# New hand-written instruction orders for a four-stage block on one core, with Pool masking three tiles and stores on two queues

## The reference, cut to what matters

```python
x = x + _L0_attn_a_ref(_layernorm(x), w1, w2, b2, sparse_mask)
x = x + _L0_ffn_ref(_layernorm(x), weight, bias, centroids, assignments)
x = x + _L0_attn_b_ref(_layernorm(x), Wqkv, bqkv, Wo, bo)
x = x + _L0_ffn_ref(_layernorm(x), weight, bias, centroids, assignments)

# stage 1
attn = jnp.einsum('ds,td->st', w1, w2) * sparse_mask
y = jnp.einsum('bds,st->bdt', x, attn) + b2;  return gelu(y)
# stages 2 and 4
dots = softmax(x @ centroids.T / 0.1)
hits = dots > 0.01
query_sel = jnp.any(hits, axis=1)      # per token
cluster_sel = jnp.any(hits, axis=0)    # over ALL tokens of all batches
row_sel = cluster_sel[assignments]     # per output feature
out = jnp.where(query_sel[:, None] & row_sel[None, :], x @ weight.T + bias, 0)
# stage 3: single-head attention with D = 128, then Wo and bo
```

## Time and profile before

| | us |
|---|---|
| median of 3 executions | 277.5 |
| lowest, highest | 277.13, 278.13 |
| profiled execution, its own time | 277.1 |
| its span in the profile | 275.3 |
| PE busy | 268.8 |
| DVE, ACT, Pool busy | 195.7, 176.6, 158.9 |
| granted TensorE clock, mean | 0.999 of full |

### The profile page before, as it was taken

The page is one execution under the profiler, slowest core; times in us unless marked ns, Lnnn a source line. Parts: engine busy times, 40 slices in busy tenths (PEclk is TensorE's granted clock), DMA queues, the critical chain, the costliest instruction groups (busy, mean ns, idle before and its releaser), DMA issues.

```text
span 275.3 us, 4427 instructions
## 1 busy us (share of the span) xinstructions
PE 268.8 (98%) x1396; PEld 224.5 (82%) x1396; DVE 195.7 (71%) x410; ACT 176.6 (64%) x358; POOL 158.9 (58%) x192
## 2 busy tenths in 40 slices
PE   8899999999999999999999999999999999999994
PEld 7787888888888888789988888888888888887673
DVE  3989988505926867775399796788349475967996
ACT  3855886455476785449899888778555567575400
POOL 4892988265495481289896993970730438113730
PEclk9999999999999999999999999999999999999999
DMA  7999064800000000000000000000000000000087
GB/s 248 368 374 317 11 228 158 304 0 0 2 0 0 2 0 2 2 0 0 2 0 0 4 1 0 0 2 0 2 2 0 0 2 0 1 2 0 19 305 287
DMA packets 10247, 18.23 MB, mean 66 GB/s; under 512 B 1201, under 2 KB 1969, under 8 KB 10225
## 3 DMA queue, kind: packets, MB, share of 16 engines
q1 hardware_dynamic: 10080, 17.70, 18.1%
q10 hardware_dynamic: 144, 0.26, 0.3%
HBM read 13.76 MB, written 4.19 MB: 65 GB/s over the span
## 4 chain that ended last, share of the span: by engine, by line
PE 92%; DVE 3%; DMA 1%; issue 1%; ACT 1%; POOL 0%; DVEq 0%; ACTq 0%; POOLq 0%
PE m_bank L977 72%; PE t_bank L1070 12%; PE m_bank L1150 5%; PE t_bank L1076 1%; DMA x_tok<-in_L_attn_a_x 1%; PE m_bank L1030 1%; DVE y_tok L936 1%; DVE qsel L908 0%; ACT ce L682 0%; DVE x_tok L960 0%; ACT xn_odd L592 0%; DVE y_tok L947 0%; PE m_bank L1097 0%; DVE st L779 0%; DVE cl L892 0%
## 5 line engine op out<-in xcount | busy, mean ns | idle before, releaser
L977 PE MATMUL m_bank<-ffn_hi,even_hi 128*128 128x512 f32 x96 | 39.0, 406 | 0.2 <-DVE y_tok L936 0.2
L977 PE MATMUL m_bank<-ffn_lo,even_hi 128*128 128x512 f32 x96 | 37.6, 392 | 0.0
L977 PE MATMUL m_bank<-ffn_hi,even_lo 128*128 128x512 f32 x96 | 37.4, 390 | 0.0
L549 POOL TENSOR_TENSOR y_tok<-y_tok,x_tok 128x512 f32<-128x512 f32 x16 | 20.4, 1297 | 25.5 <-ACT y_tok L730 25.5
L581 ACT ACTIVATE ones_and_squares<-x_tok,mv 128x512 bf16<-128x512 f32 x44 | 31.5, 717 | 4.1 <-DVE x_tok L883 3.7
L529 POOL TENSOR_TENSOR y_tok<-y_tok,bias_f 128x512 f32<-128x512 f32 x16 | 20.5, 1294 | 16.2 <-ACT y_tok L675 16.2
L457 POOL TENSOR_SCALAR ve<-mv 128x1 f32<-128x1 f32 (+1 forms) x20 | 5.3, 265 | 36.5 <-ACT ones_and_squares L581 35.5
L786 DVE TENSOR_TENSOR even_lo<-t_bank,even_hi 128x512 fp32r<-128x512 f32 x24 | 16.2, 683 | 12.8 <-ACT even_hi L624 12.6
L461 POOL TENSOR_TENSOR rstd<-ve,half 128x1 f32<-128x1 f32 (+1 forms) x31 | 23.6, 760 | 2.6
L786 DVE TENSOR_TENSOR odd_lo<-t_bank,odd_hi 128x512 fp32r<-128x512 f32 x28 | 18.8, 686 | 6.4 <-ACT odd_hi L624 6.2
L977 PE MATMUL m_bank<-odd_hi,wqkv_hi 128*128 128x512 f32 (+1 forms) x60 | 21.5, 358 | 0.0
(11 more groups left out here) (186 smaller groups left out, 776.1 us busy)
## 6 DMA issues: line engine op xcount, KB each, us to landing
out<-x_tok SPq DMA_DIRECT2D x15, 256.0 KB, 2.3
x_tok<-in_L_attn_a_x SPq DMA_DIRECT2D x3, 1024.0 KB, 8.4
xn_odd<-in_L_attn_a_xt SPq DMA_DIRECT2D x2, 1024.0 KB, 6.7
x_tok<-in_L_attn_a_x SPq DMA_DIRECT2D x4, 256.0 KB, 4.3
w_raw<-in_L_attn_a_w SPq DMA_DIRECT2D x4, 256.0 KB, 5.2
xt_other<-in_L_ffn_weight SPq DMA_DIRECT2D x4, 256.0 KB, 6.5
y_tok<-in_L_attn_a_sparse_mask SPq DMA_DIRECT2D x4, 256.0 KB, 6.9
xt_other<-in_L_attn_a_xt SPq DMA_DIRECT2D x1, 1024.0 KB, 5.2
```

Of the source, the lines that this page charges most:

```text
L549: pool.tensor_tensor(y_tok[:, n, :], y_tok[:, n, :], x_tok[:, n, :], ALU.add).then_inc(done[kind], 1)
L977: ins = pe.matmul(bank, a, w, start=(first and n == 0), stop=(last and n == count - 1))
```

## The change

All six lists are written anew, and five things are new in the code:
- Three tiles of stage 4, (1, 3), (2, 3) and (3, 2), the set `BY_POOL`, have no `xb` and no `out`. Their `blend4` waits for `qb` instead. Then Pool multiplies the tile of `y_tok` with the row mask (`pm`) and adds it to `x_tok` (`pa`), and the store waits for `pa`.
- For this the mask is made a second time: `masks.4`, one more matmul right after `mask.4`, into a `t_bank`, and `rows4` copies it to SBUF on ACT, as its last step but one.
- Seven stores and one of the two half stores go to ACT's queue, behind all of ACT's steps (`AS_ORDER`).
- `load.w1.1`, not `load.w1.0`, is the load on ACT's queue.
- `masks` belongs to the kinds that use a `t_bank`.

In the lists: the weights w1 and w2 are loaded ahead of x (the x tile that comes first is the seventh piece on SP's queue), in stage 1 PE transposes its first tile of x behind `last.1`, and the order of chunks, batches and tiles differs all through.

```diff
+BY_POOL = {(1, 3), (2, 3), (3, 2)}
...
 PE_ORDER = """
-attn.0.0 T.x1.0.0 attn.0.1 attn.0.2 T.x1.0.1 attn.1 T.x1.0.2 last.0 last.1 last.2 last.3 T.x1.0.3 y1.0.0.c0
...
+attn.0.0 attn.0.1 attn.0.2 attn.1 last.0 last.1 T.x1.0.2 last.2 last.3 T.x1.0.0 T.x1.0.1 T.x1.0.3 y1.0.2.c02
...
+AS_ORDER = """
+store.2.0 store.1.1 store.1.3 store.0.0 store.0.2 store.2.2 store.2.3 storeh.3.3.0
+"""
...
+AQ_ORDER = """
+load.w1.1
+"""
...
-T_KINDS = ("T", "tc", "bestT", "colmean", "ffnmean")
+T_KINDS = ("T", "tc", "bestT", "colmean", "ffnmean", "masks")
...
                 if kind == "store":
                     b, t = key
-                    sp.wait_ge(*done_at("out", (b, t)))
+                    if key in BY_POOL:
+                        sp.wait_ge(*done_at("pa", key))
+                    else:
+                        sp.wait_ge(*done_at("out", key))
...
+                elif kind == "pm":
+                    b, t = key
+                    n = b * TPB + t
+                    pool.wait_ge(*done_at("rows4", ()))
+                    pool.wait_ge(*done_at("blend4", key))
+                    pool.tensor_tensor(y_tok[:, n, :], y_tok[:, n, :], rows[:, :], ALU.mult).then_inc(done[kind], 1)
+                elif kind == "pa":
+                    b, t = key
+                    n = b * TPB + t
+                    pool.wait_ge(*done_at("pm", key))
+                    pool.tensor_tensor(x_tok[:, n, :], x_tok[:, n, :], y_tok[:, n, :], ALU.add).then_inc(done[kind], 1)
...
+                elif kind == "rows4":
+                    act.wait_ge(*done_at("masks", (4,)))
+                    act.wait_ge(*done_at("masked"))
+                    act.activation(rows[:, :], bank_of("masks", 4)[:, :], ACT.Copy).then_inc(done[kind], 1)
...
+            for kind, key in AS_STEPS:
+                b, t = key[:2]
+                if kind == "storeh":
...
+                if key in BY_POOL:
+                    act.wait_ge(*done_at("pa", key))
+                else:
+                    act.wait_ge(*done_at("out", key))
+                act.dma_start(out_d[b, t * P:(t + 1) * P, :], x_tok[:, b * TPB + t, :]).then_inc(stored, 16)
...
                     dve.wait_ge(*done_at("dn4", key))
-                    dve.wait_ge(*done_at("xb", key))
+                    if key in BY_POOL:
+                        dve.wait_ge(*done_at("qb", key))
+                    else:
+                        dve.wait_ge(*done_at("xb", key))
...
+                elif kind == "masks":
+                    bank = bank_for("masks", *key)
+                    pe.wait_ge(*done_at("csel", key))
+                    pe.matmul(bank[:, :], csel[:, :], onehot[:, :], start=True, stop=True).then_inc(done[kind], 1)
```

More of the change, by code:

```diff
@@ L85 @@
+cexp.4.2 lgev.4.3 qb.2.3 qb.2.0 qb.2.1 cexp.4.3 qb.2.2 qb.3.1 qb.3.0 qb.3.2 rows4 qb.3.3
 """
 DVE_ORDER = """
[L88 to L91 removed]
```

195 lines of the change are left out of this document (97 added, 98 removed).

## The result

The change takes 278.68 us (median of 20 runs, 276.97 to 280.71) against 277.21 for the kernel before (20 runs, 276.95 to 278.41) on the same chip: a ratio of 1.0039, 95% interval 1.0023 to 1.0056. Measured again later (number 10) it gave 1.0046 (1.0028 to 1.0064). It is slower, by a little over the 0.3% that can be told from nothing, where 276.1, a faster kernel, was forecast. The runs of the change are also spread over 3.7 us, those of before over 1.5.

A forecast was written before the change was run, and what follows sets the result against it. TensorE bounds the kernel, busy 268.8 of 275.3 us, with stalls almost only at both ends. Head -0.4, middle +0.1, tail -1.4 and +0.3 after PE's end sum to -1.4: median 276.1 us, range 275.0 to 278.4.

The forecast's parts named there:

- The start: Head: w2hi.0 moves from 4.91 to about 5.3 to 5.45, so PE's first product starts 0.4 us later, about 6.1.
- xt.1 at 28.1: Head: at 0.69 us a piece, xt.1 lands at 28.1, early enough that xhi.1.0's wait for it on ACT costs nothing.
- The head in sum: Head: new losses of 0.4, 0.3 and 0.3 us against old losses of 1.1 and 0.3 removed, so -0.4.
- Rival B: Head: Pool's sums run late behind ffn.0, PE waits for xlo.1.0, slower at 279.1 us; chance 0.17.
- I take +0.1: Middle: some steps have less PE work before their user, each fitting or missing by a tenth or two; +0.1 us.
- PE's tail, -1.4: Tail: all 1.6 us of PE's waits, mostly for banks blend4 frees, come back; masks.4 adds 0.23; -1.4 us.
- near 270.3: End of PE's work: a sign named for the forecast being right, against 271.46 before.
- After PE's end, +0.3: After the last matmul: DVE ends 1.7 to 1.8 us after PE against 1.55, and stores bunch; together +0.3 us.
- The stores bunch a little: +0.15: After PE's end: some stores, such as those of pa.2.3 and out.3.1, come within 0.3 us; +0.15 us.
- M: Tail: the moment mask.4 ends, from which later steps were timed; forecast 9.9 us before PE's end, not 11.8.
- Rival C: Tail: DVE's outs take 0.70 us, blends come 0.5 late, the end 0.8 later, 276.9 us; chance 0.08.
- rival D: Tail: masking by Pool and the second store queue do nothing for the time, all gain being PE's waits; no chance given.

The follow-up runs named there:

- number 13: The change with stores on SP, gelu.0.2 ahead, middle reordered, mask.4 sooner and two outs ahead of blend4.2.1: 276.68 us, 0.9979 of the kernel before.
- number 18: The change with only the tail's edit (mask.4 sooner, two outs ahead of blend4.2.1) and all stores on SP: 277.77 us, 1.0017 of the kernel before.
- number 9: The kernel before with every second store, the last half row among them, on ACT's queue: 277.47 us, 0.9999 of the kernel before.
- number 6: The change with norm.3.1.3, lo.x3.1.2 and lo.x3.1.3 moved ahead and gelu.0.2 ahead of xhi.1.0: 279.56 us, 1.0075 of the kernel before.
- number 11: The change with stores on SP, gelu.0.2 ahead of xhi.1.0, norm.3.1.3 ahead and x2.2.3 behind lo.x3.1.3: 278.01 us, 1.0022 of the kernel before.
- number 3: The change with ffn.0, ffn.3, x.1, b2 and xt.1 loaded ahead of x.3, x.2 and the biases: 281.67 us, 1.0146 of the kernel before.
- 14: The kernel of number 13 with x.3 loaded behind xt.1: 277.38 us, 0.9991 of the kernel before.
- 12: The kernel of number 11 with cl4.3.h0, tc.4.3, mask.4 and masks.4 sooner on PE: 278.42 us, 1.0013 of the kernel before.
- Numbers 4: The change with norm.3.1.3 alone moved ahead of hi.x3.1.0 and hi.x3.1.1 on ACT: 278.55 us, 1.0045 of the kernel before.
- number 5: The change with norm.3.1.3 ahead on ACT, and lo.x3.1.2 and lo.x3.1.3 ahead of x2.2.3 and max.0.0 on DVE: 279.32 us, 1.0054 of the kernel before.
- number 16: The change with all stores on SP and no masking by Pool, DVE masking the three tiles: 280.85 us, 1.0133 of the kernel before.
- number 2: Stages 1 and 2 in the change's orders, stages 3 and 4 and stores as before, no Pool masking: 278.68 us, 1.0049 of the kernel before.
- 17: The change with only the tail's edit (mask.4 sooner, two outs ahead of blend4.2.1), stores on two queues: 277.64 us, 1.0016 of the kernel before.
- number 7: Old orders for stages 1 and 2, the change's behind, lo.x3.0.0 to .3 ahead of x2.1.0, plus number 5's edits: 282.35 us, 1.0159 of the kernel before.

## Why the prediction was wrong, point by point

Three steps failed. Two lie in PE's own work, the head's landing of xt.1 (-0.4 forecast, +0.95 measured) and the middle (+0.1, and +1.1 to +1.5). They turned the sign: number 13, whose orders take out most of both waits, is 1.05 us under number 18, which has them in full (by the ratios, on two chips; their intervals just meet). The third, the stream of stores behind PE's end, took part of what the tail gave.

- **The start, "about 6.1".** 6.12 in the first trace, and by luck. w2hi.0 didn't move from 4.91 to 5.3: it ran at 4.80, and ended at 5.41. The product could have followed near 5.5, as in number 10's trace (5.53, w2hi.0 ending at 5.43). It waited for the 24 warm-up matmuls that PE runs ahead of its products. In 8 of the 20 traces, number 9's with the old order among them, these last until 6.12; in the other 12 the product starts at 5.53 to 5.80. So the 0.4 belongs to the execution, not to the order.
- **y1.0.2 waiting 0.3 for rawlo.2** didn't happen in either trace of the change.
- **Head, "xt.1 at 28.1", and "The waits on ACT (xhi.1.0 for xt.1) are covered: gelu.0.2 still ends at 29.2".** This step failed, by the landing. The forecast had gelu.0.2 behind xhi.1.0: 28.1, 0.6 and 0.5 make its 29.2. But xt.1 landed at 29.66, so that gelu.0.2 ended at 30.80 and x1.0.2 at 31.52, which PE wanted at 30.25. It wasn't issued too late: that was at 19.26, and ffn.3, ahead of it, landed at 26.96. The DMA engines were full (share 1.04 to 1.07 from 16 to 28 us). ffn.0 landed at 24.33 (forecast 24.0), ffn.3 at 26.96 (25.3); in number 10's trace they landed at 23.57 and 24.93, and xt.1 took 4.0 us behind them, not 2.8. So 0.69 a piece gives the mean and not the landing of a single load, and PE had no slack for 1.6 us. What held these pieces up isn't shown; at the end of this burst, too, one engine works alone (share 0.05 from 30.0 to 31.5 in number 10's trace, until x.2 lands at 31.50). The wait is 1.0 to 1.4 us in six of the traces, and gone with gelu.0.2 ahead of xhi.1.0 (numbers 6, 11) or with xt.1 loaded sooner (3, 14).
- **The head in sum**, by its stalls: not -0.4 but +0.95 in the first trace (0.41 for the start, 0.28 for its first matmuls, 1.43, less 1.06 and 0.11). In number 10's PE reaches the end of this stall 0.75 us sooner, so about +0.2 there; and up to 1.6 more where a weight tile lands late.
- **Rival B (Pool).** In the change's traces it fell by its own rows: 1.3 an operation, xlo.1.0 at 32.1. But it named the next wait in line: with the gelu's wait gone, y1.1.0 waits 0.3 to 1.1 us for xlo.1.0 (numbers 6, 11, 12, 13).
- **Middle, "I take +0.1".** It was +1.1 to +1.5 (+1.3 in the first trace, 1.08 and 0.24). I measured how much work of PE lies between a step and its user, and took each step to start when its inputs are there. norm.3.1.3 had its inputs; its place on ACT's queue was the cause. Numbers 4, 5 and 11 show it: moved alone it gained nothing, with max.0.0 pushed back it lost more, and with x2.2.3 behind it all but 0.3 to 0.7 us were gone (numbers 11 to 14).
- **PE's tail, -1.4.** Right: the waits of the earlier trace rows, nearly 2 us with all their restarts, are gone, for 0.23 of masks.4.
- **PE's end "near 270.3".** The forecast's own terms, -0.4, +0.1 and -1.4 from 271.46, give 269.8. It was 271.61, and 270.60 in number 10's trace.
- **After PE's end, +0.3, and "The stores bunch a little: +0.15".** The rate of the stores is no term of the sum. The step measured +0.5 in the first trace and +1.9 in number 10's, 1.4 of it the late landing. The numbers stood in my own rows: 0.69 us a piece of 256 KB, which I had used on the loads alone. Sixteen pieces to store are fifteen steps, 10.4 us. The first store is issued 1.6 us after M and lands 2.1 after that, so the last can't land sooner than 14.0 us after M. PE's end and the 3.5 behind it came to 13.4 by my own 9.9. So even the forecast's PE would have waited 0.6 us for the stores: not enough to turn the sign alone. The old kernel, whose mask comes 2.9 us sooner (258.40, not 261.28), had 2.1 us of slack in the stream; that slack can also hide late landings, as the 0.9 us of number 9's trace. Rival C had the place right and the wrong engine.
- **Masking by Pool, "priced at 0 already" (rival D).** Not settled. Without it number 16 is 1.3% worse, in my placing of the three additions, and number 2 is not. The second queue: 0 as said, in number 9 and between 17 and 18. The Trainium skill's rule on it ("DMA: Bandwidth & Descriptors", Issuing engines are not separate DMA queues) agrees: 17 and 18 differ by 0.0001.
- **In sum.** In the first trace PE's end is 0.16 later than before: head +0.95, middle +1.3, tail -1.75, and the rest by small stalls under 0.1 us, which I didn't count. With +0.5 behind it that makes +0.6 of span against the forecast's -1.4. In number 10's PE's end is 0.85 sooner and the time behind it +1.9: +1.05. The medians differ by 1.5; the late landings at both ends, which one profiled execution shows only by chance, are the likely rest, but no run here counts them.

## What to carry to other kernels

Look at what stands ahead of a step on its own engine's queue, not only at its inputs: both large new waits of the change came from such a place. At the end of a kernel, count the bytes still to be stored at the rate of the loads; if they fill the time to the last product, the first store sets the end, and work taken off TensorE behind it brings nothing. And slack in a stream of transfers is worth something by itself: an order that uses every landing at once can be faster in its best execution and slower in the median, as number 11 is (276.08 at best and 278.01 in the median, against 276.99 and 277.56 for the kernel before).

## What the runs showed of the hardware that I had not expected

- A single transfer can land late in a steady stream, of loads or stores, on either queue: by 1.4 to 1.6 us in 3 of 11 traces with the change's tail among the stores, and by 0.4 to 0.9 us a tile in numbers 3, 4 and 13 among the first weights. Where the stores end so (number 10), the last 1.4 us have a DMA share of 0.05, about that of one of the 16 engines: the others are done.
- The clock of TensorE fell from 2.4 to 1.2 GHz, for seven or eight matmuls, after 1.96 us of stall in one trace (number 6) and after 2.41 us in number 7's, and stayed up after 1.98 us in another (number 5). In number 3 it fell after stalls of 0.78 and 1.97 us, 3.5 us from one to the other. Where it falls, a stall costs nearly twice its length; the waits of 1.1 to 1.4 us in the change never brought it down in a trace. The mean clock of a run can't tell this alone: in number 10's trace it is 0.996 only because the clock falls at 274.18, behind PE's end.
- The meeting of DVE and Pool holds for tiny operations too. In the kernel before, one of 128x4 takes 1.30 us, and ends as the Pool addition does that began 0.01 before it (the same in numbers 2 and 9); others of its line take 0.17:

```profile
253.07 1.28 POOL L549 TENSOR_TENSOR y_tok<-y_tok,x_tok 128x512 f32<-128x512 f32 x1 [0.96 <-ACT y_tok L730]
...
253.08 1.30 DVE L908 TENSOR_SCALAR qsel<-crec 128x4 f32<-128x4 f32 x1
```

It shows as a longer operation, not as idle time, so the list of waits has no line for it.
